# Gate and up product by Strassen's seven products with the sums kept in PSUM, gated values in DRAM, and the down product as a pass of its own

## The reference, cut to what matters

```python
x = x + xattn(layernorm(x), ctx, Wq, bq, Wk, bk)   # scores (xWq)(ctxWk)^T / 32, softmax, times ctx
W  = NF4_CODE[q].reshape(-1, 64) * absmax[:, None]  # gate, up: (3584, 1024); down: (1024, 3584)
g  = einsum('bsh,mh->bsm', layernorm(x), Wg)
u  = einsum('bsh,mh->bsm', layernorm(x), Wu)
out = x + einsum('bsm,hm->bsh', silu(g) * u, Wd)
```

## Time and profile before

| what | value |
|---|---|
| median of 3 runs | 2277.65 us (2275.87 to 2278.98) |
| profiled execution, its own time | 2272.95 us |
| its span, first to last instruction | 2271.2 us |
| PE busy | 95% (L1451 1169.4 us, L1470 586.8 us) |
| DVE, ACT, POOL busy | 62%, 59%, 9% |
| mean granted TensorE clock | 0.989 |

### The profile page before, as it was taken

How to read it: one execution, slowest core, us unless ns; L and a number is a source line. 1 busy time by engine, 2 the same in 40 slices (tenths; PEclk the granted TensorE clock), 3 DMA queues, 4 the chain that set the end, 5 groups by cost and what they waited for, 6 DMA issues and landing times.

```text
span 2271.2 us, 33097 instructions
## 1 busy us (share of the span) xinstructions
PE 2166.7 (95%) x10934; PEld 1090.6 (48%) x10934; DVE 1405.4 (62%) x2165; ACT 1340.3 (59%) x2466; POOL 215.0 (9%) x216
## 2 busy tenths in 40 slices
PE   8879898879999999999999999999999999999998
PEld 3367777744344444444444444444444444444443
DVE  6665454686675747566575757566575758575544
ACT  4864444557856657575656566565756566665420
POOL 0021312200101000000101010000101010100000
PEclk9989999999999999999999999999999999999999
DMA  9010010012222222122222222122222222222103
GB/s 322 19 47 20 19 37 18 24 37 57 66 52 52 52 46 58 44 53 49 55 50 52 52 53 54 45 52 43 57 54 51 50 53 52 52 52 47 42 5 153
DMA packets 243497, 124.63 MB, mean 55 GB/s; under 512 B 191089, under 2 KB 219761, under 8 KB 243313
## 3 DMA queue, kind: packets, MB, share of 16 engines
q1 hardware_dynamic: 240800, 121.57, 21.7%
q10 hardware_dynamic: 2512, 0.79, 0.1%
HBM read 69.90 MB, written 8.39 MB: 34 GB/s over the span
## 4 chain that ended last, share of the span: by engine, by line
PE 71%; ACT 3%; DVE 2%; issue 2%; ACTq 0%; DVEq 0%; DMA 0%; POOLq 0%; POOL 0%; SPq 0%
PE ps L1451 47%; PE ps L1470 24%; ACT sq L187 1%; ACT sq L183 1%; DVE act_buf L1352 1%; ACT halves L218 1%; DVE y L1361 0%; DVE w L208 0%; PE ps L1439 0%; DVE xT L1340 0%; DVE halves L224 0%; DVE h L1335 0%; DMA q<-in_L_ffn_up_q 0%; ACT act_buf L1303 0%; ACT xT L1285 0%
## 5 line engine op out<-in xcount | busy, mean ns | idle before, releaser
L1451 PE MATMUL ps<-xT,wgu 128*128 128x512 f16 x5376 | 1169.4, 380 | 10.8 <-DVE xT L1340 4.5
L1451 PEld LDWEIGHTS ps<-xT,wgu 128*128 128x128 f16 x5376 | 525.9, 98 | 643.3 <-issue 12.4
L208 DVE SCALAR_TENSOR_TENSOR w<-sq,w 128x512 f32<-128x512 f32 x672 | 464.8, 692 | 350.9 <-ACT sq L187 310.5
L1470 PE MATMUL ps<-wd,h 128*128 128x512 f16 x2688 | 586.8, 380 | 24.2 <-DVE y L1361 21.4
L187 ACT ACTIVATE sq<-sq 128x512 f32<-128x512 f32 x1008 | 557.7, 616 | 0.0
L183 ACT ACTIVATE sq<-q 128x512 f32<-128x512 int32 x672 | 401.8, 620 | 161.1 <-DVE w L208 143.6
L1470 PEld LDWEIGHTS ps<-wd,h 128*128 128x128 f16 x2688 | 261.6, 98 | 347.2 <-DVE y L1361 38.0
L1361 DVE SCALAR_TENSOR_TENSOR y<-ps,y_out,y 128x512 f32<-128x512 f32 x448 | 335.4, 749 | 89.3 <-PE ps L1470 89.3
L1272 POOL TENSOR_TENSOR h<-act_buf,h 128x512 f16<-128x512 f32 x112 | 129.7, 1158 | 1651.8 <-ACT h L1309 1651.8
L224 DVE SCALAR_TENSOR_TENSOR halves<-w,halves 128x512 f16<-128x512 f32 x168 | 172.2, 1025 | 135.1 <-ACT halves L218 135.1
L1309 ACT CAST h<-act_buf 128x512 f16<-128x512 f32 x112 | 69.2, 618 | 286.6 <-DVE act_buf L1352 286.6
(11 more groups left out here) (154 smaller groups left out, 956.8 us busy)
## 6 DMA issues: line engine op xcount, KB each, us to landing
q<-in_L_ffn_down_q SPq DMA_DIRECT2D x56, 256.0 KB, 3.3
q<-in_L_ffn_up_q SPq DMA_DIRECT2D x55, 256.0 KB, 2.8
q<-in_L_ffn_gate_q SPq DMA_DIRECT2D x54, 256.0 KB, 2.8
y<-in_x SPq DMA_DIRECT2D x4, 2048.0 KB, 20.3
xT<-in_ctx SPq DMA_DIRECT2D x8, 1024.0 KB, 4.9
out<-y SPq DMA_DIRECT2D x3, 2048.0 KB, 6.6
xT<-in_L_xattn_Wq SPq DMA_DIRECT2D x8, 512.0 KB, 10.7
wk<-in_L_xattn_Wk SPq DMA_DIRECT2D x16, 256.0 KB, 11.1
```

What stands on the lines that cost most here:

```text
L208: nc.vector.scalar_tensor_tensor(out=un.w[:, slot, :], in0=un.sq[:, i % SQ_RING, :], scalar=FACTORS[i][1], in1=un.w[:, slot, :], op0=ALU.a ...
L1451: last = nc.tensor.matmul(ps[:, 2 + 2 * mat + n % 2, :], un.wgu[:, odd, mat, k // 4, a, k % 4, :], t.xT[:, n, c, k, :], start=k == 0 and j ...
L1470: last = nc.tensor.matmul(ps[:, 6 + n % 2, :], h[:, s, a, i * P:(i + 1) * P], wd[:, s, hh, c, :, :].rearrange("p k d -> p (k d)"), start=m ...
```

## The change

The weight matrices of gate and of up are each taken as 14 blocks of two chunks by two halves of the 1024 features, x as two halves of the features by two halves of each batch's tokens, and the product of the two 2x2 block matrices is made by seven block products in place of eight (Winograd's form of Strassen's method). A *stage* is gate or up of two chunks: 28 stages. A stage has seven weight *pieces*: three of the four units as they are and four sums (`combine`, DVE), all split into halves (7 casts, 7 low halves, 7 turns in place of 4). Each piece is used for two *sides* (batches 0 to 3, 4 to 7), and one *slot* is a piece by a side: 12 matmuls of 128x512. There are 392 slots. In stage 0 all of side 0 comes first, later the sides alternate. The sums of products are made in PSUM: PE goes on adding to a bank that ACT or DVE has written.

```diff
+                for k in range(SLOT_COUNT):                      # PE
+                    stage, product, side = product_at(k)
+                    if side == 0:
+                        turned(pe, un, z)
+                    if stage == 0:
+                        pe.wait_ge(t.s_T[side][product], 16)
+                    if product == P1:
+                        freed(pe, stage - 1, P2, side)
+                    if product == P6:
+                        pe.wait_ge(s_xy, 2 * stage + side + 1)
+                    if product == P7:
+                        pe.wait_ge(s_z, 2 * stage + side + 1)
+                    if product == P4:
+                        pe.wait_ge(s_v, 2 * stage + side + 1)
+                    todo = [(kt, a, b) for kt in range(4) for a, b in PARTS]
+                    for n, (kt, a, b) in enumerate(todo):
+                        last = nc.tensor.matmul(ps[:, bank, :], un.wS[:, z % SLOTS, a, kt, :], t.Tp[:, side, product, :, b, kt, :],
...
+                def after(k):                                    # ACT
+                    if product == P1:
+                        nc.scalar.copy(ps[:, Y + side, :], ps[:, X + side, :]).then_inc(s_xy, 1)
+                    elif product == P5:
+                        nc.scalar.copy(t.p5[:, side, :], ps[:, Z + side, :]).then_inc(s_p5, 1)
+                    elif stage % 2 == 0 and product in EVICTS:
+                        nc.scalar.activation(t.act_buf[e], ps[:, EVICT_BANK[product] + side, :], ACT.Silu,
...
+                def after(k):                                    # DVE
+                    if product == P6:
+                        nc.vector.tensor_tensor(ps[:, Z + side, :], ps[:, Y + side, :], t.p5[:, side, :], ALU.add).then_inc(s_z, 1)
+                    if product == P7:
+                        nc.vector.tensor_tensor(ps[:, V + side, :], ps[:, Y + side, :], t.p5[:, side, :], ALU.add).then_inc(s_v, 1)
+                    if stage % 2 and product in EVICTS:
+                        nc.vector.scalar_tensor_tensor(out=t.act_buf[e], in0=ps[:, EVICT_BANK[product] + side, :],
```

The order is P1, P5, P6, P2, P7, P3, P4. In slot k ACT does `after(k-1)`, `hidden_hi(k-2)` and then some decode steps; DVE does `after(k-1)`, `hidden_lo(k-3)` (POOL's work before) and then decode steps. How many is fixed by `Plan`, which counts steps and the waits between them:

```diff
+        if phase < HIDDEN_PHASE:
+            n = phase % ATTEND_PHASES
+            return (0, 0, 0, 2, 1, 1, 0, 0, 0, 1)[n], (1, 1, 1, 1, 1, 1, 1, 1, 1, 1)[n]
+        if phase < DOWN_PHASE:
+            k = phase - HIDDEN_PHASE
+            if k < FIRST_SLOTS:
+                return 1, 3
+            return (2 if k // SPLIT_STEPS % 2 or k % 2 else 3), 6
+        return (6, 5, 5, 6, 5)[(phase - DOWN_PHASE) % 5], 12
```

```diff
+def t_hi(nc, act, t, b, j):
+    n = PIECES * b + j
+    wait(act, t.s_tt[n % 2], 16 * (n // 2))
+    nc.scalar.copy(t.t16[:, n % 2, 0, :], t_rows(t, j)).then_inc(t.s_thi, 1)
...
+def t_turn(nc, sp, t, b, j):
+    sp.wait_ge(t.s_tlo, n + 1)
+    sp.dma_start(t.tst[:, n % 2].rearrange("p a k m -> p (a k) m"), t.t16[:, n % 2].rearrange("p a d -> p (a d)"),
+                 transpose=True).then_inc(t.s_tt[n % 2], 16)
...
+                def step(b):                                     # DVE, attend
+                    key_scales(b)
+                    if old:
+                        dve.wait_ge(s_bn, b - 1)
+                        y_scales(nc, dve, t, b - 2, link)
...
+                    softmax(b)
+                    if b < LAST:
+                        key_max(b + 1)
+                    if old:
+                        for j in range(4, PIECES):
+                            t_lo(nc, dve, t, b - 2, j)
+                    if b > 0:
+                        moments(b - 1)
+                    streams.dve.run(base + 9)
```

The gated values' halves go to DRAM (`hs`, 256 KB each), and the down product is a second pass of 112 steps: 28 chunks for each of four groups (half of the features by half of the tokens), 24 matmuls a step in eight open PSUM banks; DVE adds to y only at a group's end (32 additions in place of 448). SP's list for it:

```diff
+                for m in range(DOWN_STEPS):
+                    group, c = m // CH, m % CH
+                    load_h(m + H_RING)          # waits for the end of step m; 512 KB
+                    units_due(DOWN_PHASE + m)   # turns and loads of the plan's phase m
+                    if 1 <= c <= BANKS and group > 0:
+                        store((group - 1) * BANKS + c - 1)
+                    if BANKS < c <= 2 * BANKS:
+                        load_y(group * BANKS + c - BANKS - 1)
```

More of the change, by code:

```diff
@@ L91, in block_of @@
[L91 to L108, removed]
+Q_RING, HALF_RING, SLOTS = 3, 3, 11
+ROW_BANK, COL_BANK = 4, 3
+PARTS = ((0, 0), (0, 1), (1, 0))
+HALVES = DIM // BANK
+PRODUCTS = 7
+Y_RING = 4
@@ L228, in turn_unit @@
[L228 to L240 removed]
+        src = (t.gate_q, t.up_q)[mat][chunk * P:(chunk + 1) * P, half * BANK:(half + 1) * BANK]
@@ L241, in xattn_ffn_kernel, with __init__, run @@
+PLAN = Plan()
+class Stream:
+    def __init__(self, steps, upto):
+        self.steps, self.upto, self.done = steps, upto, 0
+    def run(self, phase):
+        while self.done < self.upto[phase]:
+            next(self.steps)
+            self.done += 1
+def xattn_ffn_kernel(nc, x, ctx, Wq, bq, Wk, bk, gate_q, gate_absmax, up_q, up_absmax, down_q, down_absmax, out, ys, xs, hs):
     with ExitStack() as whole:
@@ new lines, in t_next, with t_rest, units_due @@
+                def t_next(b, j):
+                    t_store(nc, sp, t, b, j - 2)
+                    t_turn(nc, sp, t, b, j)
+                def t_rest(b, first):
+                    for j in range(first, PIECES):
+                        t_next(b, j)
+                    for j in range(PIECES - 2, PIECES):
+                        t_store(nc, sp, t, b, j)
+                def units_due(phase):
+                    for z in PLAN.turns.get(phase, ()):
+                        turn_piece(nc, sp, un, t, z)
+                    for u in PLAN.loads.get(phase, ()):
+                        load_unit(nc, sp, un, t, u)
@@ L794, in step @@
                         last.then_inc(s_r, 1)
-                        if o == PROBS_AT and not first:
+                        if o == PROBS_AT and b > 0:
                             turn_probs(b - 1)
@@ new lines, in hidden_hi @@
+                def hidden_hi(k):
+                    stage, product, side = product_at(k)
+                    if stage % 2 and product in EVICTS:
+                        e = 2 * EVICTS.index(product) + side
+                        g = 8 * (stage // 2) + e
+                        if g == 0:
+                            act.wait_ge(t.s_tlo, PIECES * BATCH)
+                        act.wait_ge(s_h, g + 1)
+                        wait(act, s_hst[g % HST_RING], 16 * (g // HST_RING))
+                        nc.scalar.copy(t.hst[:, g % HST_RING, 0, :], t.act_buf[e]).then_inc(s_hhi, 1)
```

1473 lines of the change are left out of this document (829 added, 644 removed).

## The result

The changed kernel takes 2285.17 us in the median (2281.84 to 2290.69) against 2276.13 us before (2273.53 to 2281.68) on the same chip: ratio 1.0039, 95% interval 1.0026 to 1.0052. It is slower, by 9 us, where 2205 us were forecast. The profiled execution has a span of 2284.6 us, against 2271.2 before; the forecast span was 2198.

The account below looks back on a forecast made before the run. PE was taken to bound the feed-forward, and nearly the attention. Span 2271.2 - 14 + 54.5 + 36.5 - 151.6 + 1.5 = 2198 us, plus 1.75 and 4.7, gave 2205 us; range 2140 to 2275.

Parts of the forecast that it names:

- Matmuls: Feed-forward: 4704 gate and up matmuls at 0.2160 us, 2688 down at 0.2168; together 1598.9 us, 198.7 less.
- The rival of the gathered operand: Slots: matmuls slower with moving operand gathered from four runs of 128 columns; 7% takes the gain, 2277 us; chance 0.05.
- ACT and DVE keep up, +10 us for lags: Gate and up slots: ACT 87% and DVE 82% busy, under PE's 72.6 us per two stages; 10 us added for lags.
- it paces the down pass: Rival, down pass: later turns from SP's list cost 2 us for each of some 25 units, +50, 2255 us; chance 0.08.
- Its first rival: Up stages: ACT and DVE pace the slots, casts of h waiting for DVE; +122 us, 2327 us; chance 0.10.
- Stage 0: First gate and up stage: side 1's last piece comes 8 to 12 us late, +10 us; restart at low clock +2.
- The down pass: Down products: late turns in SP's list cost 21 us, group changes 4 us; 608 us in all.
- The three waits in steps 25 to 27: Down pass: turns issued one step ahead each wait about 4.9 us, plus 2 us of low clock; 21 us together.
- Prepare: Before the attention: without DVE's decode, statistics and low halves follow PE's own end; -14 us.
- The steps of the attention: Steps 2 to 7: ring of two delays casts and evictions; +10 each for 2 to 6, +4.5 for 7, +54.5 us.
- The end of the attention: Last scores to first slot: 43 to 53 us, taken as 50 against 13.5 before; +36.5 us.
- The parts as the prediction lists them, 20, 7, 15 and 4: Attention's end: 20 us before the product, product 7, three rounds of 5 for batch 6's forms, batch 7's scales 4.

Follow-up runs that it names:

- the last experiment: The combined version with three of side 0's seven loads ahead of batch 6's turns, four and the store of y behind: 2163.72 us, 0.9507.
- the combined version: Changed kernel with four places in `halves`, SP's turns ahead of slot stores and down-pass loads, three turned-form places, ten turned-weight slots: 2163.27 us, 0.9496.

## Why the prediction was wrong

1. *Matmuls.* Right. 4704 and 2688, at 0.216 us where nothing disturbs them. The rival of the gathered operand is refuted by the stretch of 4488. What looked like slower matmuls in the changed kernel was the clock: behind an idle time of 5.72 us at 980.89 a stretch of 5 us shows a granted clock of 0.50, the lower level of 1.2 GHz, and 13 matmuls (23 at 0.216), the next 5 us 1.00, 2.4 GHz, and 25 (stretch, PE, PEld, DVE, ACT, POOL, clock, DMA, GB/s):

```profile
981.00:986.00 5.00, 5.00 (x13) 1.65 (x12) 4.57 (x8) 4.65 (x10) 0.00 (x0) 0.50 0.65 129
986.00:991.00 5.00, 5.00 (x25) 2.29 (x24) 4.07 (x7) 5.00 (x11) 0.00 (x0) 1.00 0.29 84
```

2. *ACT and DVE keep up, +10 us for lags.* This is the step that failed. Its loads were about right: 87% and 82% forecast, 79% and 70% of the longer slots found (876.48 and 774.75 of 1110 us), which for slots of 2.59 us is 86% and 76%. But a sum of loads isn't a schedule, and +10 us for lags was a number without a row behind it. The step looked for waits between ScalarE, VectorE and PE only. It left out the loop that closes through SP: cast, low half, turn, landing, and only then the cast three pieces later. The units' chain of 14.33 us for two, from a kernel whose SP list had no stores of h in it, was carried over as it stood. Against the mean pace three places would do: PE uses three pieces in 15.5 us, and in only 6 of the 42 waits behind 640 us of the trace did a piece's loop take longer (12.4 us in the mean). But the plan lets casts come in bunches, three within 3.65 us in the example, and eight stores of h, from slot 9 of an up stage on, each waiting for the slots' own evictions, lengthen the loop there. ScalarE stands in the cast, the copy of P1 behind it comes late, and PE waits. It cost 72 us over the forecast; one more place (75 us) or another order (52 us) each removes most of it. A place of the copy ahead of the cast in ScalarE's list, or casts spread more evenly, was not tried. The prediction had said of SP's list that it paces the down pass, and didn't ask the same of the slots. Its first rival had the place (ScalarE late in up stages; PE paid at the start of the gate stage behind) and the point from which it decides (slots of 2.77 us, 2.83 came), with another mechanism: it had the casts of h wait for VectorE, and the group of those casts on the page shows 0.3 us of idle time ahead of them in all. The low halves cost 0.69 us in the slots and 0.94 in the attention beside POOL, as taken from the earlier trace rows. The Trainium skill (GPSIMD Engine Reference, Specifications), cited for this in the prediction, says that GpSimd shares its SBUF interfaces with VectorE, and the trace agrees.

3. *Stage 0.* Forecast +10 and +2. The first 11 slots, up to 599.69, took 42.3 us where their matmuls are 28.5 at 0.216, so 13.8 us more; but only 6.0 of these are waits for side 1's loads, 4.4 are a wait for a copy of P1, and the rest is the low clock. The number was near, the reason half.

4. *The down pass.* Right, and near in size (613.2, forecast 608). The order of SP's list was the cause, as said, and undoing it gave all of it back. The three waits in steps 25 to 27 came as forecast, 5.78, 5.33 and 5.19 us for 4.9, and the low clock behind them cost 2.3 to 3.0 us each for 2 (24 matmuls in 7.52 to 8.19 us, 5.2 at 0.216). Four shorter waits for the turns issued two steps ahead add 2.4 us, forecast as "nothing, just". Group changes and the start of the pass cost 2.9 us for 4.

5. *Prepare.* -19.6 instead of -14: right in sign and cause, low in size.

6. *The steps of the attention.* +60.7 forecast as +54.5, steps of 50.8 us (346.23 to 397.01, the first products of R of two steps) forecast as 50. The number held, the reason only in part. The wait for the additions to y came as forecast, 20.4 us in six steps (3.4 each for 3 to 4). PE did wait for ScalarE's eviction at the third product as well:

```profile
407.51 10.47 PE L1193 MATMUL ps<-T 128*128 128x256 f16 x72 [4.64 <-ACT T L1249]
```

but with half of that wait taken away the steps are as long, because the scaling of the keys is next in the same list, and with 4.6 us of work taken from each only 1.8 us a step come back. What in the step would have to move together for it to get shorter was not found.

7. *The end of the attention.* 60.7 instead of 50. The parts as the prediction lists them, 20, 7, 15 and 4, add up to 46 us and not to the 43 it went on with. The first held: PE's product starts 19.9 us behind the scores. The order of the loads in the queue was the right thing to look at, and was sized low: two turns took 16.33 us where with nothing left ahead they take 2.90, so 13.4 us more and not up to 10. The Trainium skill (DMA: Bandwidth & Descriptors, Queues, rings and completion order) was cited for this; it says that each DMA engine consumes descriptors in ring order. The trace agrees: 8 MB were issued from 511.21 on, at the 423 GB/s that the trace shows in this stretch they last until about 531 (an estimate), and the first turn's issue ends at 530.08; the 3 MB of the last experiment, issued from 501.02 on, were through by the same estimate before its first turn at 510.61. The term left out is the store: the forecast had three rounds of 5 us for five forms, but the ring of two for turned forms makes each turn wait 2.4 us for the store ahead of it, 3.7 us a form. A third place gave 9 of the 10.7 us back, 5.6 of them in this pitch.

So where did the expected gain go? The feed-forward before was 199 us longer than the bare matmuls of the one after (145 us by fewer matmuls, the rest waits and transposes that went). These 199 us went to the attention (41 us, with prepare's gain in it), the boundary (47), the slots (94 over their matmuls) and the down pass (30): 213 us. That is 14 more than was won; less 1 at the tail it is the 13 us between the two profiled spans. With a place more in each of two rings and SP's calls in another order in two places, 112 us of gain are left, as the combined version shows.

## What to carry to other kernels

Where the sum fills an engine to 80% or more, as here, don't stop at the sum: write down each loop that closes through a ring of buffers, with every queue it passes (here cast, low half, SP's list, landing), and hold its length against how fast the list comes back to the same place, in its densest stretch and not in the mean. Then ask what stands behind the entry that waits: PE never lacked a piece here, it lacked the copy behind the cast. In a list that one engine issues in order, what somebody waits for goes ahead of what nobody waits for; a store that waits for the present work must not stand in front of a transfer that is ready. And a wait found at one place is worth what the next wait in the same list leaves: remove one and measure before counting the gain.

## What the runs showed of the hardware

Issuing a turn on SP, 1.23 us in the median, took 12.15 us with 8 MB of loads and stores issued in the 6.7 us ahead of it, and 10.63 us with 6 MB issued in the 7.4 us ahead, about until these were through; what stands behind it in SP's list is held up as well. Seven loads of 1 MB issued one behind the other took 3.84 us. Squares of 256 columns took 404 ns where 512 took 622: half the columns is two thirds of the time. A product with its moving operand gathered from four runs of 128 columns kept 0.2159 us a matmul over 4488 in a row. And 24 matmuls behind an idle time of over 5 us took 7.5 to 8.2 us instead of 5.2.
